# Sharing a pair's six stack loads between two DMA-issuing engines in a two-layer attention and mixture-of-experts kernel

## What is computed

```
xn = layernorm(x)
s  = attention(xn)
g  = silu(mixture_of_experts(xn))
x  = x + s * g
```

## Time and profile before

| | |
|---|---|
| runs | 542.84, 543.9, 544.36 us; median 543.9 |
| the profiled execution | 546.77 us, of which the span from the first to the last instruction is 545.0 |
| busy share of the span | PE 81%, DVE 60%, ACT 35%, POOL 34% |
| issues of L704 | 120, 72 of layer 0 and 48 of layer 1, all by SP |

### The profile page before, as it was taken

How to read it: one execution, slowest core, us unless ns; L and a number is a source line. 1 busy time by engine, 2 the same in 40 slices (tenths; PEclk the granted TensorE clock), 3 DMA queues, 4 the chain that set the end, 5 groups by cost and what they waited for, 6 DMA issues and landing times.

```text
span 545.0 us, 10275 instructions
## 1 busy us (share of the span) xinstructions
PE 440.9 (81%) x3600; PEld 305.3 (56%) x3600; DVE 325.9 (60%) x831; ACT 188.7 (35%) x407; POOL 184.8 (34%) x224
## 2 busy tenths in 40 slices
PE   3456898878898998799999999765594969889960
PEld 2324666544574564477776776553573646577640
DVE  3786647799887765135331338788569566732335
ACT  1101324443444555633453323121103333454212
POOL 2333200353786214004000047243606385411324
PEclk9857979999999999999999999889567989899985
DMA  7340775466496520413332253033623747000114
GB/s 230 95 122 2 232 225 164 139 200 200 124 292 192 158 55 3 135 60 98 108 106 70 77 188 102 10 92 112 176 86 100 220 150 229 27 2 14 62 34 144
DMA packets 50492, 65.87 MB, mean 121 GB/s; under 512 B 8051, under 2 KB 41715, under 8 KB 48907
## 3 DMA queue, kind: packets, MB, share of 16 engines
q1 hardware_dynamic: 48139, 58.93, 35.5%
q0 software_dynamic: 2304, 6.29, 3.6%
HBM read 42.88 MB, written 22.02 MB: 119 GB/s over the span
## 4 chain that ended last, share of the span: by engine, by line
PE 54%; DVE 21%; POOL 7%; issue 6%; DMA 5%; SPq 3%; ACT 2%; POOLq 0%; DVEq 0%; ACTq 0%
PE bank L1010 9%; PE bank L1032 7%; PE bank L905 4%; DVE work L1471 4%; PE bank L912 4%; PE bank L808 3%; PE bank L839 3%; DMA work<-work 3%; PE bank L955 3%; PE bank L933 3%; PE bank L835 3%; POOL x_slots L1297 2%; DVE work L1435 2%; PE bank L793 2%; PE bank L1017 2%
## 5 line engine op out<-in xcount | busy, mean ns | idle before, releaser
L1471 DVE TENSOR_REDUCE work<-bank 128x4 f32<-128x512 f32 (+1 forms) x144 | 96.3, 687 | 61.1 <-PE bank L839 59.2
L1133 ACT ACTIVATE work<-bank 128x512 f32<-128x512 f32 x144 | 84.1, 595 | 105.7 <-PE bank L863 61.8
L835 PE MATMUL bank<-neg_ts,identb 128*128 128x512 bf16 (+1 forms) x144 | 49.2, 341 | 30.8 <-DVE work L1471 24.5
L1097 ACT ACTIVATE work<-bank 128x256 f32<-128x256 f32 (+4 forms) x131 | 51.5, 401 | 60.3 <-PE bank L905 20.7
L1261 POOL TENSOR_TENSOR work<-work 128x512 f32<-128x512 f32 (+1 forms) x20 | 21.3, 1064 | 109.4 <-ACT work L1097 109.2
L912 PE MATMUL bank<-work,cst 128*32 128x256 f32 (+1 forms) x768 | 52.7, 345 | 0.0
L905 PE MATMUL bank<-work 128*32 128x128 f32 (+1 forms) x704 | 49.0, 352 | 3.9 <-POOL work L1252 2.6
L1774 DVE TENSOR_TENSOR work<-work,bank 128x176 f32<-128x176 f32 x47 | 15.8, 336 | 59.6 <-ACT work L1186 59.3
L839 PE MATMUL bank<-work 96*128 96x256 bf16 (+1 forms) x320 | 50.2, 262 | 0.0
L1032 PE MATMUL bank<-moe,work 88*128 (+1 forms) x188 | 50.2, 390 | 0.0
L1010 PE MATMUL bank<-moe,work 128*128 x124 | 42.1, 462 | 0.8 <-ACT work L1097 0.5
(11 more groups left out here) (196 smaller groups left out, 772.9 us busy)
## 6 DMA issues: line engine op xcount, KB each, us to landing
moe<-w_in SPq DMA_DIRECT2D x27, 352.0 KB, 3.9
work<-q_parts SPq DMA_DIRECT2D x48, 128.0 KB, 2.6
x_slots<-wo SPq DMA_DIRECT2D x9, 512.0 KB, 3.9
work<-x_slots SPq DMA_DIRECT2D x31, 128.0 KB, 2.2
y_slots<-work SPq DMA_DIRECT2D x31, 128.0 KB, 1.7
q_parts<-work SPq DMA_DIRECT2D x8, 384.0 KB, 2.7
parts<-work SPq DMA_DIRECT2D x8, 384.0 KB, 2.8
moe<-parts SPq DMA_DIRECT2D x24, 128.0 KB, 2.6
```

The lines of the kernel that those rows point to most:

```text
L835: nc.tensor.matmul(view[:, :, half * P:half * P + P], identb[:, :], neg_ts[:, :].unsqueeze(1).to_broadcast([P, len(ms), P]), start=True, s ...
L1097: return nc.scalar.activation(dst, src, ACT.Copy)
L1133: nc.scalar.activation(pT[at % 6], a.st.bank(w)[:, :], ACT.Exp, scale=SCALE)\
L1471: nc.vector.tensor_reduce(here[:, first:first + len(ms), half], a.s.bank((b, q))[:, :].rearrange("p (m s) -> p m s", s=n), AX_X, ALU.max, ...
```

## The change

The function that loads a pair takes an engine and a list of slots. Where `shared_load` holds (all of layer 1, and batch 0 of layer 0), SP issues slots 0 to 2 and ACT slots 3 to 5, each behind its own wait for the staged parts. ACT does so at the place of `load` in its list. The semaphores that the scores wait for still count six loads.

```diff
--- before.py
+++ after.py
@@ -626,6 +626,25 @@
         block = ctx.enter_context(nc.Block())
 
 
+        def shared_load(a, b):
+
+            return a.n == 1 or b == 0
+
+        def load_slots(eng, a, b, g, slots):
+
+            n, home = pair_at(a, b, g), parts_home(a, b, g)
+            m0, m1 = pair_maps(a, g)
+            eng.wait_ge(a.staged[n % 2], 16 * (n // 2 + 1))
+            if b >= a.kept:
+
+                last = 3 if (a.n, g) == (0, 0) else a.units - 1
+                eng.wait_ge(a.st.full, a.st.at[(b - a.kept, last, 2)] + 1)
+            k_parts, q_parts = (0, 1, 2, 0, 1, 0), (0, 0, 0, 1, 1, 2)
+            for slot in slots:
+                rows = qkT[a.n][b % a.kept][slot:STACK:SLOTS, m0:m1, :]
+                eng.dma_start(rows.rearrange("p m t -> p (m t)"), home[(k_parts if g == a.key_side else q_parts)[slot]])\
+                    .then_inc(a.loaded[b % 2][g], 16)
+
         @block.sync
         def _(sp):
             x_tiles = x_d.rearrange("(t p) d -> p t d", p=P)
@@ -691,17 +710,7 @@
 
             def load(a, b, g):
 
-                n, home = pair_at(a, b, g), parts_home(a, b, g)
-                m0, m1 = pair_maps(a, g)
-                sp.wait_ge(a.staged[n % 2], 16 * (n // 2 + 1))
-                if b >= a.kept:
-
-                    last = 3 if (a.n, g) == (0, 0) else a.units - 1
-                    sp.wait_ge(a.st.full, a.st.at[(b - a.kept, last, 2)] + 1)
-                k_parts, q_parts = (0, 1, 2, 0, 1, 0), (0, 0, 0, 1, 1, 2)
-                for slot, k in enumerate(k_parts if g == a.key_side else q_parts):
-                    rows = qkT[a.n][b % a.kept][slot:STACK:SLOTS, m0:m1, :]
-                    sp.dma_start(rows.rearrange("p m t -> p (m t)"), home[k]).then_inc(a.loaded[b % 2][g], 16)
+                load_slots(sp, a, b, g, range(SLOTS // 2 if shared_load(a, b) else SLOTS))
 
             def attention(a, steps):
                 for kind, w in steps:
@@ -1110,6 +1119,8 @@
                         act.wait_ge(norms[a.n].expin, 1)
                         sc = (sc0, sc1)[a.n]
                         nc.scalar.activation(sc[:, 1, :], sc[:, 0, :], ACT.Exp).then_inc(norms[a.n].expd, 1)
+                    elif kind == "load" and shared_load(a, w[0]):
+                        load_slots(act, a, *w, range(SLOTS // 2, SLOTS))
                     elif kind == "high":
                         n, width = pair_at(a, *w), pair_width(a, w[1])
                         act.wait_ge(a.turned, n + 1)
```

## The result

**Slower: 558.05 us (median of 4 runs, 556.61 to 560.27) beside 544.13 for the kernel before on the same chip, a ratio of 1.0241 [1.0205, 1.0278].** That is +13.1 us on the 543.9 of before. The profiled execution took 560.27 us, its span is 558.5, against 545.0: +13.5 us. The lines of the changed kernel are shifted; L645 is now the load (L704 before), L708 the staging, L697 the maximum rows, L1106 ACT's copy, L1186 the Silu of finished tiles, L1197 the experts' Silu, L1144 the exponential, L1234 the power, L877 the second form of `exp` on PE.

The account below looks back on a forecast made before the run. Work alternates between engines; a pair's loads are limited by SP's issuing, and ACT's in-order holds cost more. Terms 4.75 (1.45 within it) + 3.0 + 4.4 = 12.1 us on 543.9 gave 556 us; range 552 to 561.

Parts of the forecast that it names:

- the Silu of the last expert: Sign on ACT beside the last experts: this step, held behind load and `high(0,1)`, runs 3 us later.
- the power on POOL: Sign in layer 1: the last tiles' layer-norm power comes 4.7 us later, right behind POOL's `rest`.
- The price of an issue: ACT's three issues per pair: 1.84 us, from SP's row; bounded by nothing and 3.67 us per pair.
- Layer 0's first batch: Key loads issued up to 3.8 us earlier, but DVE's layer norm covers the whole gain: 0.
- Pairs (0,0) and (0,1): Layer 1, beside the last experts: ACT's hold delays Silu, DVE's product and PE's matmul: +1.45 us.
- Pairs (1,0) and (1,1): Layer 1: held `high(1,1)` delays POOL's `rest`, the power and the maxima: +4.75 us in all, 1.45 within it.
- Pairs (2,x): Layer 1, batch 2: ACT's hold delays exp(0,1,1), whose PSUM bank PE's exp(0,2,0) needs: +3.0 us.
- Pairs (3,x): Layer 1, batch 3: ACT's hold delays the rows' copy, staging and exp(1,1,1), then PE's exp(1,2,0): +4.4 us.
- Cheap issue: Rival: ACT issues almost for nothing, only its waits remain: 546 to 552 us, chance 0.20.
- one shared issue path: Rival: two queues issue no faster together, ACT held 3.67 us per pair: 561 to 567 us, chance 0.10.
- lower bound: All terms with ACT's issues priced at nothing: 0 + 1.5 + 0 + 0.8 = 2.3 us, median 546.
- faster rival: If ACT copies batch 1's maximum rows before SP is free, they leave 1.9 us earlier: 542.0 us; chance 0.06.

Follow-up runs that it names:

- waits only: Changed kernel, but SP issues all six loads and ACT only waits at each load: 550.12 us beside 546.96, ratio 1.0079.
- later places: Changed kernel, but ACT issues layer 1's halves later in its list and layer 0 is left to SP: 545.56 us beside 546.96, ratio 0.9976.
- early pairs alone: Changed kernel, but only layer 1's batches 0 and 1 (four pairs) are shared: 549.42 us, ratio 1.0086.
- six by ACT: Changed kernel, but ACT issues all six loads of the shared pairs and SP none: 570.7 us, ratio 1.0456.
- two doses: Two runs against the changed kernel: ACT issues none of the shared pairs' loads but still waits (550.12 us), or issues all six (570.7 us).
- batch 2 alone: Changed kernel, but only layer 1's batch 2 (two pairs) is shared: 549.71 us, ratio 1.0102.

## Why the prediction was right

**The direction and the mechanism held.** ACT's list is held at each load, and what stands behind it is awaited. The waits that were named are in the trace: the Silu of the last expert 3.6 us later with its 0.5 of offset taken out (361.48 to 365.59), where 3.3 were worked out; the power on POOL right behind `rest(1,1)`, PE idle before exp(0,2,0) and exp(1,2,0) until ACT. That the sum came so near is in part luck: the terms are off to both sides, as the ladder shows (+1.7, then -1.0, +0.4 and -0.6 us).

**The price of an issue.** Taken from SP's row, 1.84 us for three. In layer 1 of this trace ACT's three take 1.78 where they do not start together with SP's (373.26), and 2.03 to 2.30 where they do. The choice of the nearest row was right to 0.2 to 0.5 us. The rule cited in the prediction (the Trainium skill, "DMA: Bandwidth & Descriptors", "Issuing engines are not separate DMA queues") has two halves: that only issue time is saved agrees, since six issues on two queues took 2.06 us instead of 3.67; that this is usually small next to the DMA doesn't carry over, since three issues of ACT, 1.78 to 2.30 us, stand beside a landing of 3.0.

**Layer 0's first batch, 0.** Measured +0.5 us within an interval that holds 0. The gain before DVE is there, 2.1 us at PE with the offset taken out, and DVE covers it.

**Pairs (0,0) and (0,1), 1.45: too small.** This is the term that was mis-sized. The ladder has 3.1. DVE's product of the last expert is 2.8 late with the offset out (362.70 to 365.99, less 0.5), PE's matmul behind it (366.38 against 364.01) 1.9. The other 1.2 us lie in what PE does next, the eight matmuls of a projection (L819, L828 now): from their start to the next group it took 1.98 us before (366.14, granted clock 0.88) and 3.21 after (368.54, 0.53), with PE busy throughout. The prediction had no term for a matmul that takes longer. That the hold is the cause of that lower clock isn't shown: the same eight took 2.13 with waits only, 2.72 with the later places, where no hold was left, 2.77 with the early pairs alone and 3.41 with six by ACT, so a part of the excess belongs to the single execution. The 1.0 us that is back by the loads of (2,0) was given back the same way: seventeen matmuls from 399.06 took 5.07 us before (granted clock 0.50) and 4.11 after (from 405.99, 0.62).

**Pairs (1,0) and (1,1), 3.3 more: the right size, with luck.** From the landing (385.12) to the power (390.92) it took 5.80 us; worked out were 5.82 (382.93 to 388.75). Two errors cancel in it: ACT's issues took 2.08 us to the start of `high` instead of 1.83, and POOL's `rest` 3.02 instead of 3.30.

**Pairs (2,x), 3.0 against 3.4.** `high(2,1)` and the staging came as worked out: 423.23 and 427.03, less the 5.96 of delay at the landing, are 417.27 and 421.07, against 417.01 and 421.0. But the staged parts landed 2.89 us after the issue, not 4.43 as before, so exp(0,2,0) was only 2.15 late (433.01 less 424.90 and 5.96) instead of 3.0. The remaining 1.3 us were lost behind it, before the loads of (3,0): from exp(0,2,0) to the next projection PE needed 3.83 us before (424.90 to 428.73, granted clock 1.00) and 5.13 now, without a pause (433.01 to 438.14, 0.67). The size was near, the way to it partly another: a shorter landing, and slower matmuls, which the prediction had not counted.

**Pairs (3,x), 4.4 against 3.8.** Less the 9.39 of delay, the rows' copy ran at 446.44 (446.3 worked out), the rows' DMA left at 446.73 (446.6), the staging at 448.69 (448.6). It landed after 2.78, not 4.18, and exp(1,2,0) came at 454.55 (455.2 worked out, 450.79 before). The landing was 1.4 shorter than worked out, ACT's issues 0.5 longer.

**The rivals.** Cheap issue and one shared issue path fall by the rows of ACTq and by the two doses; their prices, +2.3 and +23 us, stand beside the doses measured, +4.3 and +24.9. The waits alone cost more than the 2.3 us of the lower bound, and one place shows why: with SP's six issues kept, the staging of (3,1) leaves 5.62 us behind the loads of (3,0), as before (5.63), and exp(1,2,0) comes 10.45 us behind these loads (443.96 to 454.41), 7.99 before: 2.5 us late, where the bound, with SP done after three, had 0.8. Of the faster rival not only the condition failed, but also its price: where the condition was met, PE gained at most 0.35 us and not 1.9. The row of the wait, 0.16 us, gave the size better.

## What to carry to other kernels

An engine that issues a DMA in its own instruction order also takes on that DMA's wait; cost both as a hold of everything behind, and look for who awaits those steps. Halving the issue time of a queue was worth here at most about what the consumer's idle row showed as waiting for it, and nothing where another engine covered that wait. If a second issuing engine is wanted, put its issues at a place in its list where the data has already landed: here the place of layer 1's issues made some 14 us (from +13.1 to -1.3; layer 0's part, left out in the second, is within the noise by itself).

## What was not expected of the hardware

**Two queues that start together slow one of the two a little.** Where ACT's three loads do not start together with an issue of SP's they take 1.77 to 1.88 us in the run with later places, also while SP is issuing (419.29, with SP at its issues from 418.04 to 420.68). Where both queues start together in layer 1 of the changed kernel, ACT's take 2.03 to 2.30 and SP's mostly 1.75 to 1.78, but 1.95 and 2.30 at two of the places; in the run with batch 2 alone it is SP that needs 2.06 at one place (426.50) and ACT 1.78. The median landing went from 2.6 to 3.0 us; in the run with later places, where ACT's loads mostly come behind SP's, it is 2.6.

**With the holds came a lower clock.** The mean granted TensorE clock, where 1 is 2.4 GHz and 0.5 is 1.2 GHz, is 0.885 to 0.889 in the four executions of the changed kernel, 0.898 to 0.908 in the ten with later places, and 0.894 to 0.910 in the 25 of the kernel before that ran beside those. In windows of the same times the figure behind POOL's is the granted clock. Before:

```profile
361.00:372.00 11.00, 8.81 (x36) 7.22 (x37) 7.68 (x26) 2.54 (x7) 3.61 (x4) 0.84 0.54 159
414.00:437.00 23.00, 18.40 (x180) 12.70 (x181) 16.16 (x42) 7.49 (x16) 9.91 (x15) 0.78 0.65 200
```

After:

```profile
361.00:372.00 11.00, 7.98 (x22) 6.01 (x23) 6.89 (x18) 2.31 (x6) 3.80 (x4) 0.53 0.47 143
414.00:437.00 23.00, 13.98 (x149) 8.75 (x151) 13.96 (x38) 6.23 (x12) 11.38 (x16) 0.63 0.49 156
```

The work in these windows is shifted by up to 9 us, so they do not hold the same matmuls. Cut to the same number of matmuls, the clock is 0.78 before and 0.57 after for 28 of them beside the last experts (361.50 to 369.40, and 362.00 to 373.00), 0.65 and 0.66 for 152 up to batch 2 (382.00 to 413.40, and 387.00 to 420.00), and 0.78 and 0.69 for 180 from there (414.00 to 437.00, and 420.00 to 446.40). So the clock is lower where PE now waits in between, and not everywhere. Over the span the 3600 matmuls take 445.9 us instead of 440.9. On the way to the loads of (3,0) three places were seen above, +1.2, -1.0 and +1.3 us; what the clock costs in all of the 13.5 us was not separated from the waiting.
